# A weight pre-split moved behind the projection, the projection's weights in another ring, and a four-bank output transpose

## The reference, cut to what is computed

```python
xn = layernorm(x)                                  # x: (2, 8192, 1024) fp32
# attention: inside one token, over its 16 heads of 64
qkv = xn @ w_qkv.T                                 # -> q, k, v: (b, n, 16, 64)
attn = softmax(einsum('bnhd,bngd->bnhg', q, k) / 8)
o = swapaxes(einsum('bnhg,bngd->bnhd', attn, v), 1, 2).reshape(b, n, d)
att = o @ w_proj.T + b_proj
# mixture of experts: sigmoid router, top 2 of 8, plus one shared expert
r2 = relu(xn @ up[e].T) ** 2                       # 8 experts, width 512
routed = einsum('tei,ehi,te->th', r2, down, cw)
shared = relu(xn @ sup.T) ** 2 @ sdown.T           # width 2048
out = x + att + routed + shared
```

## Time and profile before

| | |
|---|---|
| the runs, us | 4377.26 and 4860.1 (median of the two 4618.68) |
| the profiled execution, us | 4386.61 |
| its span on the slowest core (core 4), us | 4385.0 |
| spans of the eight cores, us | 4338.1 to 4385.0 |
| PE busy, share of the span | 75% |
| VectorE, ScalarE busy | 24%, 13% |
| mean DMA traffic | 116 GB/s |

### The profile page before, as it was taken

How to read it: one execution, slowest core, us unless ns; L and a number is a source line. 1 busy time by engine, 2 the same in 40 slices (tenths; PEclk the granted TensorE clock), 3 DMA queues, 4 the chain that set the end, 5 groups by cost and what they waited for, 6 DMA issues and landing times.

```text
span 4385.0 us, 47046 instructions; the slowest of 8 cores (4338.1 to 4385.0 us)
## 1 busy us (share of the span) xinstructions
PE 3290.5 (75%) x16388; PEld 1809.8 (41%) x16592; DVE 1032.7 (24%) x2190; ACT 580.7 (13%) x1190; POOL 166.4 (4%) x292
## 2 busy tenths in 40 slices
PE   4566647556473738368999969999879999799997
PEld 2455535444352526253444424444334444344443
DVE  3211121221212121232222241222231222312222
ACT  1211021111102020211110011001111110110010
POOL 1001000101000000000000000000000000000000
PEclk8768766768585858668999969999889999799998
DMA  5425353545455464622222322222322222222322
GB/s 148 134 88 143 106 172 121 170 137 160 152 159 168 134 198 111 210 97 77 96 77 92 101 96 82 96 101 94 113 74 92 99 77 92 101 78 95 106 92 82
DMA packets 158292, 506.89 MB, mean 116 GB/s; under 512 B 36056, under 2 KB 36184, under 8 KB 158048
## 3 DMA queue, kind: packets, MB, share of 16 engines
q1 hardware_dynamic: 113520, 411.49, 29.7%
q0 software_dynamic: 27136, 88.16, 6.0%
q10 hardware_dynamic: 17408, 4.20, 0.9%
HBM read 411.44 MB, written 75.50 MB: 111 GB/s over the span
## 4 chain that ended last, share of the span: by engine, by line
PE 69%; DMA 11%; DVE 7%; issue 6%; ACT 4%; ACTq 2%; DVEq 0%; SPq 0%; POOL 0%; POOLq 0%
PE p L278 60%; PE p L526 3%; PE p L508 2%; ACTq L418 2%; DMA AR<-sv 2%; DMA sup_s<-AR 2%; DMA sdn_s<-AR 2%; DMA AR<-AR 2%; DVE AR L256 1%; PE p L946 1%; PE p L323 1%; DMA ssup<-AR 1%; ACT AR L252 1%; DMA ssdn<-AR 1%; PE p L859 1%
## 5 line engine op out<-in xcount | busy, mean ns | idle before, releaser
L278 PE MATMUL p<-AR,wb 128*128 128x256 bf16 (+1 forms) x9120 | 1644.3, 345 | 330.3 <-DVE AR L463 98.3
L278 PEld LDWEIGHTS p<-AR,wb 128*128 128x128 bf16 x9216 | 949.1, 104 | 1040.1 <-issue 443.3
L278 PE MATMUL p<-AR,wbig 128*128 128x512 bf16 x4516 | 1008.4, 382 | 34.8 <-DVE AR L804 27.4
L278 PEld LDWEIGHTS p<-AR,wbig 128*128 128x128 bf16 x4608 | 452.4, 98 | 588.2 <-issue 58.1
L526 PE MATMUL p<-AR 128*128 128x65 f32 x512 | 124.3, 422 | 454.2 <-ACT AR L519 454.2
L526 PEld LDWEIGHTS p<-AR 128*128 128x128 f32 x512 | 114.1, 328 | 471.1 <-issue 471.1
L885 ACT ACTIVATE AR<-AR 128x512 f32<-128x512 f32 x128 | 80.5, 629 | 1200.2 <-DVE AR L880 1200.2
L278 PE MATMUL p<-AR 128*128 128x512 bf16 x752 | 182.0, 396 | 57.2 <-DMA AR<-sv 43.2
L921 DVE TENSOR_TENSOR AR<-p,AR 128x512 f32<-128x512 f32 x128 | 88.5, 691 | 527.0 <-PE p L278 509.4
L256 DVE TENSOR_TENSOR AR<-AR 128x1024 bf16<-128x1024 f32 x96 | 117.1, 1225 | 317.5 <-ACT AR L252 317.0
L880 DVE TENSOR_SCALAR AR<-p 128x512 f32<-128x512 f32 x128 | 88.5, 692 | 355.1 <-PE p L278 355.1
(11 more groups left out here) (88 smaller groups left out, 1213.1 us busy)
## 6 DMA issues: line engine op xcount, KB each, us to landing
wb<-sup_s SPq DMA_DIRECT2D x128, 512.0 KB, 4.4
wbig<-sdn_s SPq DMA_DIRECT2D x128, 512.0 KB, 3.6
wb<-sqk SPq DMA_DIRECT2D x112, 512.0 KB, 5.4
wb<-ssup SPq DMA_DIRECT2D x64, 512.0 KB, 4.5
wbig<-ssdn SPq DMA_DIRECT2D x64, 512.0 KB, 3.6
AR<-sv SPq DMA_DIRECT2D x56, 512.0 KB, 4.3
wb<-sproj SPq DMA_DIRECT2D x56, 512.0 KB, 4.1
AR<-wup SPq DMA_DIRECT2D x32, 512.0 KB, 4.7
```

Of the source, the lines that this page charges most:

```text
L278: E.matmul(psum_ap, wa, xa_, start=(first_flag and i == 0), stop=(stop_flag and i == 2)),
```

## The change

Three edits:

1. The 16 pre-split jobs of stages 2 to 7 are moved within the stage: from before the attention inside the tokens to behind the projection, that is, to just before the next stage's V product (in stage 7: before the FFN's first layernorm).
2. The projection's weights go through `wbig` (two slots, semaphores B0 and B1) and no longer through `wb` (four slots).
3. The output transposes rotate over four PSUM banks (`p3`, `p2`, `p0`, `p1`), so that tile n waits for the addition of tile n - 4 and not of tile n - 1.

Two semaphores, G0 and G1, are added and never counted up.

```diff
@@ attention stage
-            if a >= 2:
-                for pi, (srcw, dstw) in enumerate(
-                        presplit_jobs[16 * (a - 2):16 * (a - 1)]):
-                    presplit(srcw, dstw, pi)
@@ projection
             for oc in range(8):
-                sl = oc % 4
-                dwp = load_w(wb, sl, "W%d" % sl, wproj[oc], sproj[oc], a == 0,
-                             t_wb_prev[sl])
+                sl = oc % 2
+                dwp = load_w(wbig, sl, "B%d" % sl, wproj[oc], sproj[oc], a == 0,
+                             t_wbig_prev[sl])
...
-                t_wb_prev[sl] = mmp
+                t_wbig_prev[sl] = mmp
...
             last["q_sr"] = bd.tok("T")
+            if a >= 2:
+                for pi, (srcw, dstw) in enumerate(
+                        presplit_jobs[16 * (a - 2):16 * (a - 1)]):
+                    presplit(srcw, dstw, pi)
@@ output
+            p3fin = [None] * 4
             for tsub in range(4):
...
+                pfin = [p3, p2, p0, p1]
+                pfin_tok = [last["p3"], last["p2"], last["pmm0"], last["pmm1"]]
                 for oc in range(8):
-                    W("tensor", t_rout[oc] if tsub == 0 else None, last["p3"])
+                    W("tensor", t_rout[oc] if tsub == 0 else None,
+                      pfin_tok[oc % 4] if oc < 4 else None, p3fin[oc % 4])
...
-                                E.transpose(p3[:, 0:128],
+                                E.transpose(pfin[oc % 4][:, 0:128],
...
-                                    p3[:, 0:128],
+                                    pfin[oc % 4][:, 0:128],
...
-                    last["p3"] = tfe
+                    p3fin[oc % 4] = tfe
+                last["p3"] = p3fin[0]
+                last["p2"] = p3fin[1]
+                last["pmm0"] = p3fin[2]
+                last["pmm1"] = p3fin[3]
```

More of the change, by code:

```diff
@@ L172, in build_nc @@
                     "SH", "PV", "PV2", "O0", "O1", "F0", "F1", "SW0", "SW1",
-                    "XR0", "XR1", "T", "V", "S"]
+                    "XR0", "XR1", "G0", "G1", "T", "V", "S"]
         sems = {k: _st.enter_context(nc.semaphore("s" + k)) for k in semnames}
@@ L584, in build_nc @@
                     mmp = mm_triple(pmm[sl % 2][:, 0:TA],
-                                    wsl(wb, sl, m), wsl(wb, sl, m, True),
+                                    wsl(wbig, sl, m), wsl(wbig, sl, m, True),
                                     o_mq_hi[:, TA * m:TA * m + TA],
@@ L973, in build_nc @@
         for k in ("I", "X", "W0", "W1", "W2", "W3", "WV0", "WV1", "B0", "B1", "SH", "PV",
-                  "PV2", "O0", "O1", "F0", "F1", "SW0", "SW1", "XR0", "XR1"):
+                  "PV2", "O0", "O1", "F0", "F1", "SW0", "SW1", "XR0", "XR1",
+                  "G0", "G1"):
             bd.W("gpsimd", (k, bd.cnt[k]))
```

## The result

| | before | after |
|---|---|---|
| median of the runs, us | 4387.18 (10 runs) | 4604.47 (11 runs) |
| lowest run, us | 4377.26 | 4438.93 |
| profiled execution, us | 4386.61 | 4438.93 |
| span of the slowest core, us | 4385.0 | 4437.4 |
| ratio after to before | | 1.0115, 95% interval 1.0060 to 1.0171 |

By the ratio the change makes the kernel 1.15% slower. In 8 of the 11 runs (10 of all 14 that were made) the cores of one die or of both had a lower granted clock than in the profiled execution, which happens to the kernel before too (4860.1 among its runs), and the ratio leaves such runs out. My 4429 us was 10 us under the profiled execution; my range, 4375 to 4495, did not hold the median.

What follows compares the result with a forecast made beforehand. TensorE's waits for Exp behind the pre-split, a serial block of about 65 us per attention stage, were taken as the bound. -376 + 390 + 68 + 31 - 71 = +42 us on 4386.6 gave 4429 us, range 4375 to 4495.

Steps and rivals of the forecast that it cites:

- the sum of the terms: Whole kernel: -376 + 390 + 68 + 31 - 71 = +42 us on the profiled execution, 1.0% slower.
- Removed, -376: Attention of stages 2 to 7: without the pre-split in front, TensorE's long waits for Exp become ordinary ones, -376 us.
- The gap before the V product, 75.4 us five times: After the projection in stages 2 to 6: TensorE idles 75.4 us until the next V product's weights land.
- The V product's cold start, 2.7 us: V product after each gap: TensorE starts at half clock for 5.4 us, losing 2.7 us; with the gaps +390.
- The argument that pauses between blocks don't slow them: V product: today's 1.5 us pauses between blocks don't slow the blocks; raised against the half-clock rival.
- Stage 7, +68: End of stage 7: the FFN's first layernorm waits for the pre-split's subtractions and for `x_res`, +68 us.
- The two slots of the projection, +31: Projections of seven stages: with two slots, loads wait for the product two before, +31 us (23 to 52).
- The output, -71: FFN output tiles: four banks shorten each of four phases from 31.4 to 13.7 us, -71 us (-60 to -76).
- I forecast one like the profiled: Whole kernel: the forecast is for an execution like the profiled one, 4386.6 us, not the two-run median, 4618.68.
- within 2%: Whole kernel: the change makes no difference beyond about 2% (88 us), chance 0.76.
- The half-clock rival: V products after the gaps stay at half clock, 41.1 us for eight blocks, 53 us more over five stages; chance 0.14.
- the 4482 us: Whole kernel's time if V products stay at half clock, 2.2% more than before; what the skill's rule would give.

Runs made afterwards that it cites:

- the repetition: The changed kernel run again with no edit, alternating with the kernel before: median 4447.86 us over 6 runs, ratio 1.0135.
- spread kernel with the wide wait: The spread kernel, but every load of split weights again waits for all earlier scratch writes: three of four runs at 4458.15 to 4486.83 us.
- spread kernel: Kernel before with edit 3, each stage's pre-split dealt out job by job on four slots, and attention-stage loads waiting only for stage 0's scratch writes: 4004.63 us, ratio 0.9124.

## Why the prediction was right, and where it failed

By its own steps, on the profiled execution (slowest core), where the sum of the terms was +42 and +52 was measured (+56.5 on the die medians):

- **Removed, -376.** Right: 454.2 - 78.0 = 376.2, and -376 once more when the block was taken out altogether.
- **The gap before the V product, 75.4 us five times.** Right: 74.8, 73.0, 74.2, 78.6 and 75.5, mean 75.2. In sum the wait for V weights grew by 371 us against my 377.
- **The V product's cold start, 2.7 us.** It is there, on average smaller. The windows of stage 3's V product after the gap (stretch, length, busy us of five engines, PEclk, DMA share, GB/s):

```profile
753.00:757.00 4.00, 3.01 (x8) 1.09 (x9) 0.00 (x0) 0.00 (x0) 0.00 (x0) 0.50 0.28 95
757.00:760.00 3.00, 3.00 (x10) 1.11 (x9) 0.00 (x0) 0.00 (x0) 0.00 (x0) 0.63 0.00 0
760.00:763.00 3.00, 2.22 (x11) 0.91 (x10) 0.00 (x0) 0.00 (x0) 0.00 (x0) 1.00 0.50 175
763.00:770.00 7.00, 6.24 (x29) 2.50 (x27) 0.00 (x0) 0.00 (x0) 0.00 (x0) 1.00 0.53 160
```

  At 0.50 (1.2 GHz) for some 5 us, at 1.00 (2.4 GHz) behind it, with the pauses for weights of 0.3 to 2.0 us still to come: the first 24 matmuls took 7.90 us instead of 5.34, and the eight blocks 28.8 (753.99 to 782.74) in all against 27.9. Over the five stages the first pairs lost 10.3 us, 2.1 each. Two V products had a slow block later on (timeline of TensorE). Stage 4's paused for 2.17 us before its last block, which took 4.09 us instead of 2.75; stage 5's paused for 4.46 us behind its first pair, and the next pair took 8.02:

```profile
1037.86 4.09 PE L278 MATMUL p<-AR 128*128 128x512 bf16 x12 [2.17 <-DMA AR<-sv]
...
1274.89 6.88 PE L278 MATMUL p<-AR 128*128 128x512 bf16 x24 [74.22 <-DMA AR<-sv]
1286.24 8.02 PE L278 MATMUL p<-AR 128*128 128x512 bf16 x24 [4.46 <-DMA AR<-sv]
1295.11 5.12 PE L278 MATMUL p<-AR 128*128 128x512 bf16 x22 [0.85 <-DMA AR<-sv]
```

  In all the five V products took 148.6 us from first to last matmul where before they took 137.7. That is +11, against my 5 x 2.7 = 13.5. The argument that pauses between blocks don't slow them came from one V product. Others of the same trace of before show that they can, as the one behind stage 2's projection:

```profile
756.09 7.03 PE L278 MATMUL p<-AR 128*128 128x512 bf16 x23 [2.49 <-DMA AR<-sv]
```

- **Stage 7, +68.** 93.8 - 21.3 = 72.5.
- **The two slots of the projection, +31.** A projection lasted 28.5 to 30.7 us in stages 1 to 7, around the upper edge of the 27 to 30 forecast; before, 23.0 to 24.0. The seven together took 42 us more, inside 23 to 52 and the largest miss of a term. The waits alone are 34.8 us, 26 of them, nearly four a stage where the sum had three. Alone the edit was +34 on the die medians.
- **The output, -71.** -63 on the die medians; 31.4 to 16.1 us in the first FFN stage and 13.1 in the last. The limit was named rightly, the writes' time to landing mis-sized, 6.6 us and not 5.3.

So the mechanism was right and the terms were near. Their misses, from 11 us too few for the projection to 6 too many for the gaps, partly cancel, and it is in part luck that the sum lies only 10 us under the slowest core's.

**What failed** is the step from the sum to the forecast time: "I forecast one like the profiled". The measured time is the median of all runs, 4604.47 us, 109 us above the top of the range. The sum stands on the profiled execution, and for the way from there to the median it has no term, that is, it puts it at nothing, although the prediction itself had just read 5% between the two for the kernel before (4386.61 and 4618.68). Measured, that way was 165.5 us in this group of runs (4604.47 against a profiled 4438.93) and 4.3 us in the repetition (4447.86 against 4443.52), where the median lies inside the range. What makes an execution of the same kernel take longer is not shown by any run; the cause stays open. A range that holds medians as far apart as these would have been the honest one; the terms of the sum need not change for it.

The chances: "within 2%" had 0.76, and the ratio is within, 1.0060 to 1.0171. The half-clock rival had 0.14 and fell: no V product was near the 41 us that it needed, the longest took 32.8. The Trainium skill, TensorE: Matmul & The Clock Gate, section "HAM oscillation — how this bites in real kernels", describes blocks of work that are shorter than the wait for the next weights, each of which then starts cold. The V products of the changed kernel don't meet that condition, so the 4482 us should not have been put to it: their blocks take 2.75 us and the waits between them 0.16 to 2.17 us, but for the one of 4.46, and behind that one the trace agrees. The slow block behind the 2.17 us wait is not covered by it. In the spread kernel with the wide wait the condition is met and the trace agrees: pairs of blocks of 5.4 us warm, waits of 10 to 12 us, and 7.3 to 8.1 us for a pair.

## What to carry to other kernels

A block of background work isn't made cheaper by moving it as a block: it costs what stands behind it in each queue, and the new place must be read for that queue by queue, the issuing queue of the loads first. To hide it, deal it out in single steps between the other work of the same queues, with its loads issued a step ahead, here on four slots in place of two. And let a load wait only for the write of the block that it reads: in the spread kernel the wide wait decided between 4005 and about 4460 us, in the one with the block moved it was worth 29 to 45.

## What the runs showed of the hardware

- Eight PSUM-to-SBUF additions of 128x128 fp32 run in 1.97 us when four banks let them follow each other, 0.25 each, though a single one is booked with 0.29: I had taken 0.33 from the transposes.
- A 512 KB transfer had no one duration: the loads of V weights landed in 3.5 us (median) in the changed kernel, 4.0 with edit 1 alone and 4.3 before; the Q/K loads took 5.4 before and 8.1 in the spread kernel; output writes of the changed kernel 2.9 to 9.2.
- Pauses of 4.46 us and of 10 to 12 us between blocks of TensorE were followed by slow blocks (8.02 us for 5.34 of V, 7.3 to 8.1 for 5.4 of Q/K). Pauses under 1.9 us between the blocks of a V product were not. Of about 2 to 3 us both kinds are in the traces of before and of the changed kernel: 2.17, 2.49 and 2.95 us were followed by slow blocks, 2.01, 2.18 and 2.46 were not, so the length of a pause alone doesn't decide there.
